# A ring of four token buffers, the first heads' operands loaded in two parts, and the last group finished on VectorE

## The reference

```python
x = L0_attn_content                                   # (2, 2048, 256)
Q = (x @ Wq).reshape(b, n, 16, 16)                    # K and V alike
scores = einsum('bqhd,bkhd->bhqk', Q, K) / sqrt(16)
alpha = softmax(scores, axis=-1)                      # over all keys,
alpha = where(causal, alpha, 0)                       # masked after it
x = layernorm(x + einsum('bhqk,bkhd->bqhd', alpha, V).reshape(b, n, d))
probs = softmax(x @ router_weight.T); top 2 of 8 experts, capacity 1280
expert_out = (pre * silu(gate)) @ ff_post_act_weight  # per expert
x = layernorm(x + weighted sum of the two experts)
```

## Time and profile before

| | us |
|---|---|
| median of three executions | 1772.72 |
| the profiled execution, its own time | 1772.7 |
| its span (first to last instruction) | 1770.9 |
| stage 1 and the turn, to the first score | 0 to 111.8 |
| attention | 111.8 to 1049.7 |
| router, experts and last normalisation | 1049.7 to 1770.9 |
| busy over the span: PE, ACT, DVE, POOL | 1639.9, 1260.0, 1143.5, 278.2 |
| mean granted clock of TensorE | 0.971 |

### The profile page before, as it was taken

One profiled execution on the slowest core, in us unless ns is written; L12 is line 12 of the kernel. 1 busy time (PEld: TensorE's weight loads), 2 busy tenths in 40 slices (PEclk: granted clock), 3 DMA queues, 4 the chain that ended last, 5 costly groups with the idle time before them and its releaser, 6 DMA issues. The chain is left out here.

```text
span 1770.9 us, 31343 instructions
## 1 busy us (share of the span) xinstructions
PE 1639.9 (93%) x12802; PEld 955.4 (54%) x12802; DVE 1143.5 (65%) x1765; ACT 1260.0 (71%) x1357; POOL 278.2 (16%) x231
## 2 busy tenths in 40 slices
PE   7779999999999999999999965599999999999996
PEld 6633333333333333333333322488988998889985
DVE  6657787777776877778777766635454444545466
ACT  7679999999999999999999964424243242433424
POOL 1000000000000000000000010133423415334244
PEclk9969999999999999999999988799999999999998
DMA  5994060240600603206010007023222314323143
GB/s 186 251 213 122 1 86 1 26 61 1 74 13 1 86 2 48 39 1 86 2 48 1 1 25 237 19 58 72 56 69 53 107 15 112 74 55 106 13 131 118
DMA packets 77933, 118.23 MB, mean 67 GB/s; under 512 B 8818, under 2 KB 61851, under 8 KB 77774
## 3 DMA queue, kind: packets, MB, share of 16 engines
q1 hardware_dynamic: 62880, 98.32, 24.2%
q0 software_dynamic: 14880, 17.82, 5.7%
q10 hardware_dynamic: 32, 0.07, 0.0%
HBM read 80.22 MB, written 40.37 MB: 68 GB/s over the span
## 5 line engine op out<-in xcount | busy, mean ns | idle before, releaser
L828 DVE TENSOR_REDUCE sums<-expq 128x1 f32<-128x1536 f32 (+7 forms) x576 | 558.9, 1033 | 182.6 <-ACT expq L804 182.3
L804 ACT ACTIVATE probs<-scores 128x1536 f32<-128x1536 f32 (+1 forms) x384 | 509.8, 1482 | 8.3 <-PE scores L725 8.3
L804 ACT ACTIVATE expq<-scores 128x1536 f32<-128x1536 f32 x320 | 447.6, 1538 | 2.2 <-PE scores L725 0.6
L745 PE MATMUL o_ps<-probs,v 128*32 128x256 f32 (+1 forms) x4864 | 348.6, 368 | 0.0
L725 PE MATMUL scores<-aq,ak 98*128 98x512 bf16 (+3 forms) x1280 | 304.6, 353 | 8.3 <-PEq L577 6.8
L1475 ACT ACTIVATE gate<-up_ps 128x512 f32<-128x512 f32 x128 | 76.6, 598 | 327.0 <-PE up_ps L1289 327.0
L725 PE MATMUL scores<-ak,aq 98*128 98x512 bf16 (+3 forms) x1184 | 265.1, 343 | 22.6 <-ACT probs L804 16.9
L725 PEld LDWEIGHTS scores<-aq,ak 98*128 98x128 bf16 x1280 | 95.2, 98 | 212.7 <-ACT expq L804 76.4
L1289 PE MATMUL up_ps<-xeT_hi,wup_hi 128*128 128x512 f32 x512 | 203.2, 397 | 4.6 <-issue 2.7
L1803 DVE TENSOR_TENSOR mid<-up_ps,gate 128x512 f32<-128x512 f32 x128 | 88.4, 690 | 177.2 <-ACT gate L1475 174.4
L1289 PE MATMUL up_ps<-xeT_lo,wup_hi 128*128 128x512 f32 x512 | 202.2, 395 | 0.0
(11 more groups left out here) (243 smaller groups left out, 1908.8 us busy)
## 6 DMA issues: line engine op xcount, KB each, us to landing
raw<-w_T SPq DMA_DIRECT2D x16, 1024.0 KB, 6.8
split_dram<-parts SPq DMA_DIRECT2D x48, 256.0 KB, 3.5
aq<-split_dram SPq DMA_DIRECT2D x48, 256.0 KB
ak<-split_dram SPq DMA_DIRECT2D x48, 256.0 KB
raw<-wg_T SPq DMA_DIRECT2D x8, 1024.0 KB, 5.1
v_dram<-vst SPq DMA_DIRECT2D x8, 544.0 KB, 5.4
v<-v_dram SPq DMA_DIRECT2D x8, 544.0 KB, 23.7
xT<-x_T SPq DMA_DIRECT2D x8, 512.0 KB, 5.5
```

The costliest lines, as they stand in the source:

```text
L745: last = nc.tensor.matmul(o_ps[g % O_RING][32 * h:32 * h + 32, col:col + w], value(gg, k, h, 32), probs[:, m % 2 * GH + h, at:at + w], sta ...
L804: nc.scalar.activation(dst, src[:, 0:w], ACT.Exp, scale=HD ** -0.5).then_inc(exp_done, 1)
L828: last = nc.vector.tensor_reduce(sums[:, gg % 2, col, h:h + 1], expq[:, at % X_RING, lo:lo + w], AX.X, ALU.add)
```

## The change

1. `xT` becomes a ring of four. The loads of x(2) and x(3) are issued with the first two, and step `n` loads `x(n + 4)`.
2. ScalarE's wait for POOL's fills (`none_ready`) moves from the head of its stream to the first block's copy of values. ScalarE's loop is written out for all eight blocks, VectorE's for batch 0.
3. Group 0's operands are loaded by `load_columns` in parts: head 0 whole in step 4, the other heads' first 512 columns and the shifts in step 5, the values in step 6, and the other heads' columns 512 to 2047 after the last block's stores. The last part counts on `a_loaded[1]`; TensorE waits for it at the slot of key tile 1, head 1 (t = 8), and group 1's loads wait for it on SyncE.
4. The last group is finished by VectorE outside the table: the sums of tile 38, the copy of the output, the sums of tile 39, the turned copy, the division, and the addition to `x_sb`, which was POOL's.

```diff
+        def load_columns(sp, aq, ak, heads, cols, done):
+            for s, (part, times) in enumerate(AQ):
+                for r in range(times):
+                    at = (0, 3, 5)[s] + r
+                    sp.dma_start(aq[at * HD:(at + 1) * HD, heads, cols], heads_of(split_dram[0, part], 0)[:, heads, cols]).then_inc(done, 16)
+            for at, k in AK:
+                for part in range(k):
+                    sp.dma_start(ak[(at + part) * HD:(at + part + 1) * HD, heads, cols], heads_of(split_dram[1, part], 0)[:, heads, cols]).then_inc(done, 16)
...
+        XR = 4
-            xT = sb(st, "xT", [P, 2, DC, BLK])
+            xT = sb(st, "xT", [P, XR, DC, BLK])
...
                 load_x(1)
+                load_x(2)
+                load_x(3)
...
-                    if n + 2 < NB:
+                    if n + XR < NB:
                         sp.wait_ge(x_split, DC * (n + 1))
-                        load_x(n + 2)
+                        load_x(n + XR)
...
                     if n == NG:
-                        load_queries(sp, aq0, 0, a_loaded[0])
+                        load_columns(sp, aq0, ak0, slice(0, 1), slice(0, N), a_loaded[0])
                     if n == NG + 1:
-                        load_keys(sp, ak0, 0, AK[0:1], a_loaded[0])
                         load_shifts(sp, aq0, 0, a_loaded[0])
+                        load_columns(sp, aq0, ak0, slice(1, GH), slice(0, BLK), a_loaded[0])
                     if n == NG + 2:
-                        load_keys(sp, ak0, 0, AK[1:3], a_loaded[0])
                         load_values(sp, v4_0, 0, v_loaded[0])
...
+                load_columns(sp, aq0, ak0, slice(1, GH), slice(BLK, N), a_loaded[1])
...
+                    if (b, i, j) == (0, 0, 0):
+                        act.wait_ge(none_ready, 4)
...
-                act.wait_ge(none_ready, 4)
                 split_w(0)
...
-                with act.Fori(0, NB // 2 // B) as i:
-                    for j in range(2):
-                        one_block(0, i, j)
-                for n in range(NB // B):
-                    one_block(1, n // 2, n % 2)
+                for n in range(NB):
+                    one_block(n // (NB // B), n % (NB // B) // 2, n % 2)
...
+                sp.wait_ge(a_loaded[1], 16 * A_DMAS)
                 load_queries(sp, aq[1], 1, a_loaded[1])
...
-                for gg in range(NGP):
+                for gg in range(NGP - 1):
                     pool.wait_ge(group_done, gg + 1)
...
+                        if gg == 0 and t == AT["K", 1, 1]:
+                            pe.wait_ge(a_loaded[1], 16 * A_DMAS)
...
+                last = NGP - 1
+                sum_up(last, NQS - 2, 0)
+                take(last, NG - 1, 0)
+                sum_up(last, NQS - 1, 0)
+                gather(last, NG - 1, 0)
+                finish(last, 0, 0)
+                dve.wait_ge(group_done, NGP)
+                cols = x_sb[:, NT:TT, (GPB - 1) * GH * HD:GPB * GH * HD]
+                nc.vector.tensor_tensor(cols, cols, attn[:], ALU.add).then_inc(attn_added, 1)
```

More of the change, by code:

```diff
@@ L301, in program @@
         U = 2 * DC
-        xT_loaded = [sem(f"xT_loaded{j}") for j in range(2)]
+        XR = 4
+        xT_loaded = [sem(f"xT_loaded{j}") for j in range(XR)]
         w_loaded = [sem(f"w_loaded{m}") for m in range(3)]
@@ L370, in load_x @@
                 def load_x(n):
-                    sp.dma_start(xT[:, n % 2], xT_view[:, :, n * BLK:(n + 1) * BLK]).then_inc(xT_loaded[n % 2], 16)
+                    sp.dma_start(xT[:, n % XR], xT_view[:, :, n * BLK:(n + 1) * BLK]).then_inc(xT_loaded[n % XR], 16)
                 def load_w(m):
@@ L458, in split_w, with split_x @@
                     nc.scalar.activation(w[0][:, m], w_in[:, m], ACT.Copy).then_inc(w_hi, 1)
-                def split_x(pair, j):
-                    act.wait_ge(xT_loaded[j], pair * 16 + 16)
+                def split_x(n):
+                    act.wait_ge(xT_loaded[n % XR], n // XR * 16 + 16)
                     for c in range(DC):
-                        nc.scalar.activation(x[0][:, j, c, :], xT[:, j, c, :], ACT.Copy).then_inc(x_hi, 1)
+                        nc.scalar.activation(x[0][:, n % 2, c, :], xT[:, n % XR, c, :], ACT.Copy).then_inc(x_hi, 1)
                 def one_block(b, i, j):
-                    if not (b == B - 1 and isinstance(i, int) and i + 1 == NB // 2 // B and j == 1):
-                        split_x(i + (b * (NB // 2 // B) + j), 1 - j)
+                    if b * NB // B + 2 * i + j + 1 < NB:
+                        split_x(b * NB // B + 2 * i + j + 1)
                     if b > 0:
@@ L488, in one_block @@
                                              ACT.Copy).then_inc(v_read, 1)
[L490 removed]
                 split_w(0)
[L492 removed]
+                split_x(0)
                 split_w(1)
                 split_w(2)
[L495 to L499 removed]
+                for n in range(NB):
+                    one_block(n // (NB // B), n % (NB // B) // 2, n % 2)
                 act.wait_ge(norm_read, 3 * NB + 3 - 1)
@@ L514, in split_w, with split_x @@
                     nc.vector.tensor_tensor(w[1][:, m], w_in[:, m], w[0][:, m].bitcast(FP32), ALU.subtract).then_inc(w_split, 1)
-                def split_x(pair, j):
+                def split_x(n):
                     for c in range(DC):
-                        dve.wait_ge(x_hi, pair * (2 * DC) + (j * DC + c + 1))
-                        nc.vector.tensor_tensor(x[1][:, j, c, :], xT[:, j, c, :], x[0][:, j, c, :].bitcast(FP32), ALU.subtract).then_inc(x_split, 1)
+                        dve.wait_ge(x_hi, n * DC + c + 1)
+                        nc.vector.tensor_tensor(x[1][:, n % 2, c, :], xT[:, n % XR, c, :], x[0][:, n % 2, c, :].bitcast(FP32), ALU.subtract).then_inc(x_split, 1)
                 def one_block(b, i, j):
-                    if not (b == B - 1 and isinstance(i, int) and i + 1 == NB // 2 // B and j == 1):
-                        split_x(i + (b * (NB // 2 // B) + j), 1 - j)
+                    if b * NB // B + 2 * i + j + 1 < NB:
+                        split_x(b * NB // B + 2 * i + j + 1)
                     hi, mid, lo = ([parts[:, s, u, bass.ds(i * (2 * BLK) + j * BLK, BLK)] for u in range(U)] for s in range(3))
@@ L553, in _ @@
                 split_w(0)
-                split_x(0, 0)
+                split_x(0)
                 split_w(1)
                 split_w(2)
-                with dve.Fori(0, NB // 2 // B) as i:
-                    for j in range(2):
-                        one_block(0, i, j)
+                for n in range(NB // B):
+                    one_block(0, n // 2, n % 2)
                 bound_batch(0)
@@ L593, in _ @@
                         sp.wait_ge(shift_stored[b], 16)
-                    sp.wait_ge(a_loaded[0], 16 * (A_DMAS + 1))
+                    sp.wait_ge(a_loaded[0], 16 * (2 * A_DMAS + 1))
+                    sp.wait_ge(a_loaded[1], 16 * A_DMAS)
                     with sp.Fori(0, NH) as n:
@@ L771, in _ @@
                     if gg < NGP:
-                        pe.wait_ge(a_loaded[gg % 2], 16 * (A_DMAS + 1) * (gg // 2 + 1))
+                        pe.wait_ge(a_loaded[gg % 2], 16 * (A_DMAS + 1) * (gg // 2 + 1) + 16 * A_DMAS)
                     if gg < 2:
@@ L865, in _ @@
                 measured = 0
-                for gg in range(NGP + 1):
+                for gg in range(NGP):
                     for back, work, x, i in DVE_ORDER:
@@ L869, in _ @@
                             WORK[work](gg - back, x, i)
-                        if gg > GPB and gg < NGP and work == "sum" and x % 5 == 4 and measured < NT:
+                        if gg > GPB and work == "sum" and x % 5 == 4 and measured < NT:
                             if measured == 0:
```

## The result

| | before | after |
|---|---|---|
| median (executions) | 1772.66 us (4) | 1760.24 us (4) |
| from to | 1772.59 to 1776.18 | 1758.73 to 1762.32 |
| profiled execution, its span | 1772.7, 1770.9 | 1762.3, 1760.5 |
| first score | 111.79 | 100.73 |
| first score to last product | 928.60 | 930.53 |

The ratio after to before is 0.9923, 95% interval 0.9909 to 0.9936, that is 11.3 to 16.1 us less. Forecast were 14.4 us (1758.3) in a range of 1755.5 to 1766. The profiled execution is the slowest of its four. On another chip the changed kernel ran again beside before: 1759.98 against 1773.43, ratio 0.9925 (0.9912 to 0.9938). That second profile helps to tell what belongs to the kernel and what to one execution.

A forecast was written before the change was run, and what follows sets the result against it. Bounds were waits outside steady attention: late block 7 tokens, the turn to attention, the start and attention's end. 13.0 + 2.0 - 0.6 = 14.4 us off 1772.7 gave 1758.3 us; own range 1756.0 to 1760.5, 8-in-10 range 1755.5 to 1766.

The forecast's parts named there:

- Start: First token split, without ScalarE's wait for POOL's fills: from 8.42 to 5.5, 2.9 us earlier, moving all projection blocks.
- The loops: Writing out ScalarE's and VectorE's projection loops: costed at nothing, hidden by TensorE's 9.5 us per block.
- Ring of four: Projections: ScalarE's 12.8 us token wait goes; block 7 is ready to store 13.3 us earlier, 16.2 with the earlier start.
- Loads in two parts: Turn to attention: twelve more SyncE issues before the first barrier, 6.0 us; scores start at 98.8, 13.0 us earlier.
- rival 1: Turn to attention: a full DMA queue holds SyncE's last operand issues, scores 7.1 us later, 1765.4 us; chance 8%.
- The queue's own time: DMA queue: last operand loads take 13.5 us at 131 GB/s plus 2 us to signal, landing about 110.3; margin 1.4 us.
- rival 2: Key tile 1 of head 1: last operand loads late at 109 GB/s, a 3.5 us stall, 1761.2 us; chance 20%.
- 0.6 us of stall: TensorE's added wait at key tile 1 of head 1: 0.6 us lost, bounds 0 and 3.6.
- Last group: End of attention: VectorE's 0.90 us wait goes and the addition moved from POOL saves 1.1 us, together 2.0 us.
- one of the prediction's signs of being wrong: Attention, first score to last product, 928 us: prediction wrong if it changes by more than the wait for the last loads.

The follow-up runs named there:

- the start alone: Kernel before with only ScalarE's wait on POOL's fills moved and the two loops written out, ring of two: 1769.58 us, ratio 0.9975.
- the parts alone: Kernel before with only group 0's operand loads in parts and the two loops written out, ring of two: 1767.09 us, ratio 0.9954.
- the ring alone: Kernel before with only the token ring of four and the two loops written out, operand loads as before: 1771.5 us, ratio 0.9983.
- end alone: Kernel before with only the last group finished on VectorE and the two loops written out, ring of two: 1770.37 us, ratio 0.998.
- part 3 behind the barrier: Changed kernel with the last twelve operand loads issued after the second barrier: 1764.3 us, ratio 0.9903; in a later series 1759.26 us, 0.9922.

## Why the prediction was right, and where it was off

| step | forecast | after | again |
|---|---|---|---|
| first split of tokens | 5.5 | 5.20 | 5.41 |
| block 7's first matmul | 76.9 | 76.50 | 76.83 |
| its stores issued from | 86.2 | 85.76 | 86.09 |
| all seven of them | 4.3 us | 5.7 | 5.1 |
| part 3's twelve issues | 6.0 us | 6.7 | 6.7 |
| then to the first score | 2.3 us | 2.5 | 2.4 |
| first score | 98.8 | 100.73 | 100.44 |
| part 3 landed | 110.3 | 107.6 | 105.8 |
| TensorE asks for it | 111.7 | 113.7 | 113.0 |
| stall there | 0.6 us | 0 | 0 |
| end of attention | 2.0 us | 2.2 | 2.2 |

- **Start** was right in both profiles of the changed kernel: 3.2 and 3.0 us against 2.9. In the run of the start alone the tokens landed later and the split began at 6.07; the 3.3 us at its first score hold something of the written-out loops too.
- **The loops**, put at nothing, moved block 3's stores by 0.7 us, and part 1 went out at 55.92 and not at 57.0. In the changed kernel TensorE's pace sets block 7, so nothing on its path rests on that.
- **Ring of four**: the times were right, block 7 within 0.4 us of its forecast and at full clock. The attribution was not: with two buffers the parts alone leave a wait of 3.8 us of the 12.8, and the ring alone gave 1.8 to 2.5 us at the first score, not most of the 13. What the ring gives on top of the parts no run shows, since none took it out of the changed kernel.
- **Loads in two parts**: the term that was mis-sized. I costed SyncE's issues at the rate that they had in a queue that keeps up: 4.3 and 6.0 us. They took 5.1 to 5.7 and 6.7 us, 1.6 to 2.1 us more, and that is the whole lateness of the first score. It is rival 1 in small: the backlog holds SyncE, by 2 us and not by 7.
- **The queue's own time** I took too long: part 3 landed 2.7 and 4.5 us before 110.3. It moved at 148 and 167 GB/s and not at 131, and the signal came 0.8 us behind the last bytes where the sum had 2, a term for which the prediction names no row. TensorE asked 1.3 to 2.0 us later, so the margin was 6 to 7 us and not 1.4. So rival 2, with the highest chance beside the forecast, did not come, nor did the 0.6 us of stall.
- **Last group**: 2.2 us in both, and 2.2 in the run with it alone, against 2.0.
- **Attention** kept its length: 928.18 in the second profile, 928.60 before. In the first it took 930.53, 1.9 us more without any wait for part 3, which by the letter is one of the prediction's signs of being wrong; the second profile speaks against that. The 1.9 us are thus of that execution; a clock that rose later is 0.5 of them, and a pause of TensorE in group 6 (at 820.7 us) about another 1.1. Four other profiles have one of 0.7 to 0.9 us in that group, before and the second profile of the changed kernel none over 0.2; why is open.

By the second profile the parts are 11.3 us at the front, 0.4 in attention and 2.2 at its end, 13.9 in all, less 1.1 in the last stage, where the kernel is unchanged. The forecast's 14.4 was 13.0 at the front, 0.6 of stall against it and 2.0 at the end. The front was 1.7 us too much, and the stall, which did not come, hid 0.6 of that: this part of the closeness is luck. The rest lies within what executions differ by.

What stays open: why a backlog slows SyncE's issues by this much and not another amount. No run varied the queue's depth. Whether the wait for stored parts could stand behind the barriers, so that the first score need not wait for the last store, wasn't tried, since stage 2 writes where the stored parts lie.

## What to carry to other kernels

A DMA that is moved ahead of a barrier costs the issuing engine's time there, and more of it behind a backlog, whichever queue that is from; put it behind the barrier and wait for each piece only where it is first read. A short stall of TensorE near the rise of its clock costs more than its length (2.2 and 2.6 us of stall, 4.1 us of attention), so finer waits at the first tiles can be worth as much as an earlier start. When two edits free the same wait, do each alone before saying which one did it, and look for what the single runs have in common beside their edit.

## What the runs showed of the hardware

- *Issues behind a backlog.* Six stores of 256 KB took 3.6 us to issue at 61.40 and 5.6 us at 78.78 in the same kernel; six 144 KB loads took 3.9 us directly behind seven stores and 2.7 us behind the barrier.
- *The clock after a start.* In block 0, 13 matmuls ran at the 1.2 GHz level before, but 9, 12 and 7 in the runs of ring, parts and end alone, although TensorE's first matmul stood at the same 10.6 us in all. Each is 0.2 us dearer. It is not the edits: two traces of part 3 behind the barrier, the same program in this stage, have 12.2 and 11.35 us from the first matmul to block 1, 0.9 us apart. Over the runs of this case block 1 came up to 1.2 us earlier than before by the clock alone. Of the first scores something alike holds: 11.9 us after the first score the clock rose in the one profile of the changed kernel, about 14 us in the other. A difference of 1 us at such places need not be the edit's.
- *The clock after a stall.* The fall after the 2.64 us stall, just as the clock had risen (the products ahead of it took 0.70 us; 1.08 at the lower level, 0.64 at the full one), was not expected: 3.0 us of clock on top of the stall. Behind the stall of 2.17 us it was 1.5.
